# Gated scores with keys on partitions, made onto the turned probabilities, in a gated-attention and feed-forward layer

## The reference

```python
q, k, v = h @ Wq, h @ Wk, h @ Wv                   # h = layernorm(x); 32 heads of q, 8 of k and v, D = 128
qs, ks_ = softmax(q, -1), softmax(k, -1)
gs = log_sigmoid(k) / 16
# branch 1, a scan over all positions:
S = S * exp(g_t)[..., None] + k_t[..., None] * v_t[..., None, :];  o_t = q_t @ S
# branch 2: rope(q), rope(k), softmax over a sliding window (W = 64: own block and the one before)
x = x + layernorm((0.5 * y + 0.5 * o_lin) @ Wo)
# feed forward; every 64 values of w1, w2, w3 share one maximum
absmax = max(abs(w.reshape(-1, 64)), 1); n = w / where(absmax == 0, 1, absmax)
dq = NF4_CODE[searchsorted(bounds, n)] * absmax
x = x + layernorm((silu(hx @ dq1.T) * (hx @ dq2.T)) @ dq3.T)   # hx = layernorm(x)
```

## Time and profile before

| what | value |
|---|---|
| median of 3 runs | 1913.04 us (1912.93 to 1913.94) |
| the profiled execution's own time | 1912.8 us |
| its span | 1911.0 us |
| TensorE busy | 1834.3 us, 96% of the span |
| VectorE | 1484.2 us, 78% |
| ScalarE | 1278.5 us, 67% |
| GpSimd | 1264.8 us, 66% |
| DMA | 47 GB/s over the span |

### The profile page before, as it was taken

How to read it: one execution, slowest core, us unless ns; L and a number is a source line. 1 busy time by engine, 2 the same in 40 slices (tenths; PEclk the granted TensorE clock), 3 DMA queues, 4 the chain that set the end, 5 groups by cost and what they waited for, 6 DMA issues and landing times.

```text
span 1911.0 us, 42834 instructions
## 1 busy us (share of the span) xinstructions
PE 1834.3 (96%) x11439; PEld 1212.8 (63%) x11439; DVE 1484.2 (78%) x3980; ACT 1278.5 (67%) x4967; POOL 1264.8 (66%) x1164
## 2 busy tenths in 40 slices
PE   4899999999999999999999999999989999999997
PEld 3567667676777677667767776776666654444443
DVE  5999899999999888899998889999999956302112
ACT  5688777777777777777777777777677745312121
POOL 2767777777777777777777777777766738212121
PEclk8999999999999999999999999999999999999999
DMA  6101111111111111111111111111211033000000
GB/s 223 54 30 44 38 50 48 46 44 46 45 45 43 43 48 43 43 43 43 43 44 50 43 43 43 43 43 35 85 31 30 24 110 111 34 1 22 0 22 22
DMA packets 85452, 90.51 MB, mean 47 GB/s; under 512 B 14216, under 2 KB 56456, under 8 KB 85384
## 3 DMA queue, kind: packets, MB, share of 16 engines
q1 hardware_dynamic: 85384, 89.71, 15.2%
HBM read 76.48 MB, written 13.18 MB: 47 GB/s over the span
## 4 chain that ended last, share of the span: by engine, by line
PE 49%; DVE 23%; issue 19%; POOL 4%; ACT 2%; DVEq 1%; DMA 0%; POOLq 0%; ACTq 0%
PE bank L1369 12%; PE bank L1398 6%; PE bank L1358 5%; DVE f_s L1061 5%; PE bank L1340 4%; PE bank L1414 4%; PE bank L1496 3%; PE bank L1407 3%; PE bank L1435 3%; DVE f_nrm L1048 2%; PE bank L1324 2%; DVE qtT L961 2%; POOL hl L600 2%; PE bank L1514 2%; DVE qc L909 2%
## 5 line engine op out<-in xcount | busy, mean ns | idle before, releaser
L554 POOL TENSOR_TENSOR f_acc<-f_acc,f_s 128x512 f32<-128x512 f32 x429 | 548.9, 1279 | 32.6 <-POOL f_acc L554 0.4
L1369 PE MATMUL bank<-wh,xh 128*128 (+2 forms) x1024 | 335.0, 327 | 7.5 <-DVE cumh L1210 6.3
L1369 PE MATMUL bank<-wl,xh 128*128 (+2 forms) x1024 | 335.0, 327 | 0.0
L1369 PE MATMUL bank<-wh,xl 128*128 (+2 forms) x1024 | 334.8, 327 | 0.0
L1061 DVE TENSOR_SCALAR f_s<-f_nrm 128x512 f32<-128x512 f32 x480 | 282.1, 647 | 3.5
L538 POOL TENSOR_TENSOR pr<-pr,rp 128x512 f32<-128x512 f32 x128 | 133.3, 1041 | 216.1 <-DVE rp L983 216.1
L651 ACT ACTIVATE qe<-bank,nqm 128x128 f32<-128x128 f32 x512 | 180.9, 365 | 95.7 <-DVE qs L912 84.0
L1496 PE MATMUL bank<-xh,w 128*128 (+3 forms) x704 | 218.4, 379 | 1.7 <-ACT sg L837 1.7
L600 POOL TENSOR_TENSOR hl<-hf,hh 128x512 f16<-128x512 f32 (+1 forms) x44 | 51.3, 1167 | 231.4 <-ACT hh L843 231.4
L1220 DVE SCALAR_TENSOR_TENSOR hf<-bank,sg 128x512 f32<-128x512 f32 (+1 forms) x44 | 30.3, 689 | 221.5 <-PE bank L1496 210.6
L1358 PE MATMUL bank<-wh,oT 128*128 (+1 forms) x512 | 194.0, 379 | 4.4 <-DVE xl L1127 3.6
(11 more groups left out here) (179 smaller groups left out, 4918.9 us busy)
## 6 DMA issues: line engine op xcount, KB each, us to landing
f_blk<-wa SPq DMA_DIRECT2D x33, 320.0 KB, 2.9
f_raw<-wb SPq DMA_DIRECT2D x33, 256.0 KB, 2.7
dequantised<-f_w SPq DMA_DIRECT2D x33, 256.0 KB, 2.0
w<-dequantised SPq DMA_DIRECT2D x33, 256.0 KB, 4.3
raw_qkv<-wq SPq DMA_DIRECT2D x29, 256.0 KB, 2.4
raw_o<-wo SPq DMA_DIRECT2D x29, 256.0 KB, 2.6
f_recb<-scales SPq DMA_DIRECT2D x99, 64.0 KB, 2.6
f_absb<-scales SPq DMA_DIRECT2D x99, 64.0 KB, 2.6
```

The source lines that it names most:

```text
L554: nc.gpsimd.tensor_tensor(f_acc[:], f_acc[:], f_s[:, step, :], ALU.add).then_inc(s["f_ad"], 1)
L1369: last = nc.tensor.matmul(dst, av, w[:, sl + c, lo:hi], start=(n == 0), stop=(n == 3 * NC - 1))
```

## The change

The gated scores are made with keys on partitions and queries on columns, as the turned probabilities are. So they are added onto these by TensorE: the four transposes of `pr` open an accumulation in X1, and two products (keys as weights, 256 query columns each) add to it. The first takes its keys from `ktF`, a new tile that holds the first 64 keys of a tile and zeros behind them. `merge` becomes one product with a 0/1 mask from X1 to `pa`; the bias matmuls and `copy_pa` go, and ScalarE copies 64 columns more (`ktF`). `probabilities` moves from behind the state's update to ahead of `gla_scores`, which stands ahead of the turn of q as before; it waits for `softmax_p` and for the earlier `pa`. On VectorE `add_out` stands ahead of `merge`, and `nf4_end` behind `p_max`. `em` is made by ScalarE as exp(x + keep) with keep 0 or -1e30, ahead of the exponential of `ked` in the turn after a p = 0 tile. Each NF4 block gets a 65th value, the smallest normal fp32 number, and the instruction that replaced a zero maximum by 1 goes. Left out of the diff below: tiles, semaphores and start values (`cum` now lies in the staging tile; one more memset at the start, for `ktF`), and the same order of calls in the peeled last turns.

```diff
@@ -662,6 +664,9 @@
                 wait_tile(act, s["qt_d"], t, 2)
                 wait_tile(act, s["sr_d"], t, 1)
                 nc.scalar.activation(edT[:, r, :], SM[:, P:P + 130], ACT.Exp)
+                if t.p == 0 and not (isinstance(t.i, int) and t.i == 0):
+                    nc.scalar.activation(em[:, 0, :], SM[:, 2 * P:2 * P + 1], ACT.Exp,
+                                         bias=keep[:].unsqueeze(2)[:, t.i % 2, :])
                 nc.scalar.activation(ked, ked, ACT.Exp, scale=-1.0).then_inc(s["dec_ev"], 1)
 
             def mask_scores(t):
...
@@ -685,15 +690,10 @@
 
-            def copy_pa(t):
-                wait_tile(act, s["pt_done"], t)
-                wait_tile(act, s["o_done"], t, 2)
-                if number(t) == 0:
-                    act.wait_ge(s["wo_lo"], NC)
-                nc.scalar.activation(pa[:, t.p % 2, :], X1[:], ACT.Copy).then_inc(s["pa_ev"], 1)
-
             def copy_ktT(t):
                 wait_tile(act, s["ktT_done"], t)
+                wait_tile(act, s["at_done"], t, 1)
+                nc.scalar.activation(ktF[:, 0:WIN], SM[:, 0:WIN], ACT.Copy)
                 nc.scalar.activation(ktT[:, t.p % 2, :], SM[:, 0:P], ACT.Copy).then_inc(s["ktT_ev"], 1)
...
@@ -985,13 +982,10 @@
 
                 wait_tile(dve, s["at_done"], t)
-                wait_tile(dve, s["pn_p"], t)
-                v = pr[:, t.p % 2, :]
-                half = lambda a: a.rearrange("p (h n) -> p h n", h=GRP)[:, 0:2, 0:WIN]
-                nc.vector.scalar_tensor_tensor(out=half(v), in0=half(X1[:]), scalar=0.0, in1=half(v),
-                                               op0=ALU.max, op1=ALU.add)
-                nc.vector.scalar_tensor_tensor(out=v[:, 2 * P:], in0=X1[:, 2 * P:], scalar=0.0, in1=v[:, 2 * P:],
-                                               op0=ALU.max, op1=ALU.add).then_inc(s["pm_d"], 1)
+                wait_tile(dve, s["o_done"], t, 2)
+                if number(t) == 0:
+                    dve.wait_ge(s["wo_lo"], NC)
+                nc.vector.tensor_tensor(pa[:, t.p % 2, :], X1[:], cau[:], ALU.mult).then_inc(s["pa_ev"], 1)
 
             def state(t):
...
@@ -1003,9 +997,6 @@
                 if nxt.p == 0:
-                    nc.vector.tensor_tensor(em[:, 0, :], scale, keep[:, nxt.i % 2:nxt.i % 2 + 1] if isinstance(nxt.i, int)
-                                            else keep[:].unsqueeze(2)[:, nxt.i % 2, :], ALU.mult).then_inc(s["em_d"], 1)
-                    dve.wait_ge(s["em_d"], nxt.i)
                     scale = em[:, 0, :]
...
@@ -1026,15 +1017,10 @@
                     dve.wait_ge(s["f_rowd"], j)
-                nc.vector.tensor_reduce(f_col[:, 0:NF4_MAXIMA], f_blk[:].rearrange("p (b n) -> p b n", n=BLK), AX.X, ALU.max,
+                nc.vector.tensor_reduce(f_col[:, 0:NF4_MAXIMA], f_blk[:].rearrange("p (b n) -> p b n", n=GUARDED), AX.X, ALU.max,
                                         apply_absolute_value=True).then_inc(s["f_maxd"], 1)
                 dve.wait_ge(s["f_maxd"], j + 1)
-
-                nc.vector.scalar_tensor_tensor(out=f_safe[:], in0=f_col[:, 0:NF4_MAXIMA], scalar=0.0,
-                                               in1=f_col[:, 0:NF4_MAXIMA], op0=ALU.is_equal, op1=ALU.add)\
-                    .then_inc(s["f_safed"], 1)
-                dve.wait_ge(s["f_safed"], j + 1)
-                nc.vector.reciprocal(f_col[:, NF4_MAXIMA:2 * NF4_MAXIMA], f_safe[:]).then_inc(s["f_recd"], 1)
+                nc.vector.reciprocal(f_col[:, NF4_MAXIMA:2 * NF4_MAXIMA], f_col[:, 0:NF4_MAXIMA]).then_inc(s["f_recd"], 1)
 
...
@@ -1138,20 +1124,20 @@
                 if l1.real():
                     q_sums(l1)
-                if t.p == 1 and not (isinstance(t.i, int) and t.i == 0):
-                    nf4_end(t.i - 1)
                 if t.p == 2 and not (isinstance(t.i, int) and t.i == 0):
                     nf4_low(t.i - 1)
                 if l1.real():
                     gla_k(l1)
+                if l3.real():
+                    add_out(l3)
                 if l2.real():
                     merge(l2)
-                if l3.real():
-                    add_out(l3)
                 if l2.real():
                     state(l2)
                 if l1.real():
                     p_max(l1)
+                if t.p == 1 and not (isinstance(t.i, int) and t.i == 0):
+                    nf4_end(t.i - 1)
                 log_decay(t)
                 low_decay(t)
...
@@ -1328,18 +1314,11 @@
                 r = t.p % 2
                 wait_tile(pe, s["qt_d"], t)
                 wait_tile(pe, s["ktT_ev"], t)
-                wait_tile(pe, s["pa_ev"], t, 1)
-                half = lambda a: a.rearrange("p (h n) -> p h n", h=GRP)[:, 0:2, 0:WIN]
-                nc.tensor.matmul(half(X1[:]), identb[:], half(cau[:]), start=True, stop=False)
-                nc.tensor.matmul(X1[:, 2 * P:], identb[:], cau[:, 2 * P:], start=False, stop=False)
-                for b in range(2):
-
-                    keys = (b + 1) * WIN
-                    for hp in range(2):
-                        j = 2 * b + hp
-                        last = nc.tensor.matmul(X1[:, j * P:j * P + keys],
-                                                qtT[:, r, b, 2 * hp:2 * hp + 2, :].rearrange("p h n -> p (h n)"),
-                                                ktT[:, r, 0:keys], start=False, stop=(j == 3))
+                for b, keys in enumerate((ktF[:], ktT[:, r, :])):
+
+                    last = nc.tensor.matmul(X1[:, b * 256:(b + 1) * 256], keys,
+                                            qtT[:, r, b].rearrange("p h n -> p (h n)"),
+                                            start=False, stop=(b == 1), skip_group_check=True)
                 last.then_inc(s["at_done"], 1)
 
             def project_out(t):
...
@@ -1402,9 +1381,11 @@
                 r = t.p % 2
-                wait_tile(pe, s["pm_d"], t)
+                wait_tile(pe, s["pn_p"], t)
+                wait_tile(pe, s["pa_ev"], t, 1)
                 for j in range(GRP):
-                    last = nc.tensor.transpose(X1[:, j * P:(j + 1) * P], pr[:, r, j * P:(j + 1) * P], ident[:])
+                    last = nc.tensor.matmul(X1[:, j * P:(j + 1) * P], pr[:, r, j * P:(j + 1) * P], ident[:],
+                                            start=(j == 0), stop=False, is_transpose=True, skip_group_check=True)
                 last.then_inc(s["pt_done"], 1)
...
@@ -1454,12 +1435,12 @@
                 if l3.real():
                     project_out(l3)
                 if l2.real():
+                    probabilities(l2)
                     gla_scores(l2)
                 if l1.real():
                     turn_q(l1)
                 if l2.real():
                     inter_and_update(l2)
-                    probabilities(l2)
                 if l1.real():
                     scores(l1)
                 if x_tile_at(n):
...
@@ -1587,10 +1568,11 @@
-    n = np.arange(P)[:, None] % WIN
-    cau = np.zeros((P, 2, 2, P), np.float32)
-    for b in range(2):
-        cau[:, b] = np.where(n + b * WIN >= slot, 0.0, -3e38)[:, None, :]
+    key = np.arange(P)[:, None]
+    query = np.arange(WIN)[None, :]
+    cau = np.zeros((P, 2, GRP, WIN), np.float32)
+    cau[:, 0] = ((key >= WIN) | (query >= key))[:, None, :]
+    cau[:, 1] = (query + WIN >= key)[:, None, :]
...
@@ -1600,15 +1582,16 @@
-    keep = np.ones((P, 2), np.float32)
-    keep[:, 0] = 0.0
+    keep = np.zeros((P, 2), np.float32)
+    keep[:, 0] = MASKED
     return {"cosc": cos, "sinc": sin, "winmask": win, "causal": cau, "cumsum": cum,
             "identc": np.eye(P, dtype=np.float32), "keepc": keep}
 
 
 def feed_forward_pieces(w1, w2, w3):
 
-    by_block = np.zeros((NF4_PIECES, P, NF4_MAXIMA, BLK), np.float32)
+    by_block = np.zeros((NF4_PIECES, P, NF4_MAXIMA, GUARDED), np.float32)
+    by_block[..., BLK] = SMALLEST
```

More of the change, by code:

```diff
@@ L38 @@
 BLK = 64
+GUARDED = BLK + 1
+SMALLEST = float(np.finfo(np.float32).tiny)
 NF4_PIECE = 512
@@ L184, in layer @@
         win = sb("win", [P, 2, 512], BF16)
-        f_blk = sb("f_blk", [P, NF4_MAXIMA * BLK])
+        f_blk = sb("f_blk", [P, NF4_MAXIMA * GUARDED])
         f_raw = sb("f_raw", [P, NF4_PIECE])
@@ L196, in layer @@
         cau = sb("cau", [P, 512], BF16)
-        cum = sb("cum", [P, 130])
         cumh = sb("cumh", [P, 130], F16)
@@ L204, in layer @@
         ktT = sb("ktT", [P, 2, P])
+        ktF = sb("ktF", [P, P])
         krT = sb("krT", [P, 4, WIN])
@@ L218, in layer @@
         rp = sb("rp", [P, 2, GRP])
-        f_safe = sb("f_safe", [P, NF4_MAXIMA])
         PQ, PKV, X0, X1, SC, SM, PO, PW = bank
@@ L225, in layer @@
         stage = f_s[:].rearrange("p a n -> p (a n)")
+        cum = stage[:, 3840:3970]
         w_raw = [raw_qkv[:]] + [stage[:, 1536 + 768 * j:2304 + 768 * j] for j in range(NC - 1)]
@@ L246, in layer @@
             kmx_d nkm_a kabs_ev kneg_d krope_d g_d gl_d rks_d kt_d qmx_d nqm_a qrope_d rq_d qt_d pmx_d
-            rp_d pm_d pa_ev su_d em_d sr_d acc_d qrope_p krope_p qn_p pn_p
```

(25 more changed lines are left out.)

## The result

The changed kernel takes 1900.82 us (1900.40 to 1901.28, 4 runs), against 1912.99 us for the kernel before in the same session: ratio 0.9936, 95% interval 0.9918 to 0.9953. It is faster, by 12 us, and not by the 38 that were forecast. The profiled execution's span is 1898.6 us.

A forecast was written before the change was run, and what follows sets the result against it. TensorE's own work was taken to set the pace, with late VectorE adding about 1.1 us per four turns. Savings of 1.4 us in 24 steps (33.6), plus 3 and 1.5, gave 38 us: 1912.8 to 1875, range 1861 to 1894.

The forecast's parts named there:

- TensorE's work and order: Attention turn on TensorE: 0.20 us less, 11.29 to 11.09; gated scores' products in 0.87, wait for `qtT` at A+0.44.
- The new wait: VectorE, from p=3 to p=0: `gh` would wait 0.23 us for `kabs`.
- `em` on ScalarE: In p=1, `em` costs ScalarE 0.31 us, or up to 0.86, hidden behind its wait for the turn of q.
- `kt` in p=1: `kt` ends at A+2.0, or 2.3 with VectorE's later start, needed at 2.61: no TensorE stall.
- Ends: Turns outside the 24 steps: 3 us gained before 227 us and 1.5 in the last 15 turns.
- VectorE's work: VectorE per four turns: merge +0.07 us a turn, `em` -0.86, guard against zero -0.2; net -0.8 us.
- what becomes of the waits: Stalls per four turns: p=0 still loses 0.4 us, p=1 none; `nf4_end` delays L551, costing VectorE some 0.6 us.
- room: VectorE's waits for TensorE's scores, 0.46 us in 72 turns, taken as slack that absorbs lateness.
- The prediction's own sign of being wrong: Wrong if products exceed 0.95 us, `em` shows before `kt`, or VectorE no longer waits for scores in most turns.
- L551 holds VectorE: Rival: GpSimd's first sum blocks VectorE in p=1 for its whole 1.27 us; 14 us more, 1889 us; chance 0.08.
- only TensorE's work goes: Rival: ScalarE's chain, 0.25 us later every turn, eats what p=1 gives; gain 21 us, 1892 us; chance 0.18.

The follow-up runs named there:

- e12: Changed kernel with VectorE's threshold steps covering 8 of 512 columns from the second step of four turns on, GpSimd's sums all 512: 1863.79 us.
- e11: Changed kernel, nothing left out, with threshold steps reading 3 rows of 172 columns with gaps and writing one run of 516: 1852.81 us.
- e9: Kernel before the change with only `nf4_end` moved behind `pmx`: 1920.13 us.
- e3: Changed kernel with `nf4_end` put back ahead of `kt`: 1890.85 us.
- e1: Changed kernel with GpSimd's sums of the threshold steps cut to 8 of 512 columns: 1831.75 us.
- e10: Changed kernel with VectorE's threshold steps made a plain copy without two-port mode, thresholds left out: 1851.56 us.
- e13: Kernel before the change with threshold steps reading 3 rows with gaps and writing one run, nothing left out: 1946.51 us.

## Why the prediction was wrong, point by point

- *TensorE's work and order*: right. An unstalled turn is 11.09 us, the two products take 0.87.
- *The new wait, and `em` on ScalarE*: right, 0.22 us in 47 turns; `em` takes 0.30 us there and is hidden.
- *`kt` in p=1*: right. It runs from 837.00 us, A+2.0, to A+2.35 (forecast 2.3), and TensorE loses nothing in that turn.
- *Ends*: outside the 24 steps, 12.2 - 24 x 0.3 = 5 us were gained, 4.5 forecast. A small misreading: a step of before is 46.28 us and its fourth turn 11.29, not 46.32 and 11.33.
- *What failed is the step "VectorE's work"*, with "what becomes of the waits": the interval from `pmx` to the next `kmx` was taken over as 7.46 us, and the steps in it as a fixed price. It is 8.34 us now (815.55 to 823.89), where 7.46 and the new wait of 0.23 were expected, and it begins at A+4.23 and not 3.93. These 0.95 us are what lies between the 0.23 that the prediction had ahead of p=0 and the 1.18 that were lost. The dear price is that of meeting a sum of GpSimd, and VectorE's waits for the scores, which the prediction called room, were what pushed its steps behind the sums. The prediction's own sign of being wrong came true with that: VectorE no longer waits for the scores. With the scores earlier and that wait gone, the steps of p=2 and p=3 moved 1.2 and 0.6 us toward the sums and grew by 0.94 and 0.57 us. I priced this meeting for L551 alone: 0.6 us of VectorE a step, and it was 0.64; the other 1.7 of the 2.35 had no term. Part of it went into room that VectorE had; 1.1 us a step came out as time, 45.97 instead of 44.9, and 24 of them are the 26 us that are missing.
- *The rivals*: "L551 holds VectorE" had the right mechanism, in one turn of the three, and with 1889 us was 12 off; "only TensorE's work goes", with the wrong one, was 9 off. That it is an exclusion and not a slowing e12 shows. The trace of before held it too, in the ends of its 48 dear steps and of `em`, though none of the prediction's rows did. The Trainium skill's rule (SBUF — State Buffer, Who interferes with whom), that the later of the two blocks until the first has ended, agrees: 1.25 us for 8 columns, and `f_nrm` and GpSimd's rotation change places as payer with their order. Its condition agrees too: with the two-port mode of the steps prevented by outermost counts of 3 and 516 (the Trainium skill, VectorE: DVE Perf Modes, What auto-detection actually checks), e11 has one price.
- *Was it the scores' new order or `nf4_end`?* Both. The move costs 7 us alone (e9) and 10 on top of the rest (e3). e3 still misses the forecast by 16 us, as the steps of p=2 and p=3 stay at 2.82 and 4.02; e1, e10 and e11 take that away as well. Of the 94 us between e13 and e11, 68 are 24 x 2.8 in the steady steps, and some 11 more come from a turn of 15.06 instead of 13.39 us in 7 of these steps, whose cause stays open; the rest lies in the first and last turns and was not traced.

## What to carry to other kernels

A duration in a trace belongs to its neighbours as well: where two engines shut each other out, ask of every wait that a change removes what it kept apart, and price an instruction at both of its values. When one form of an instruction is half as fast but shares nothing, it can be the better one: steps of 0.61 us always, for 0.35 or over 1 (0.71 on average), were worth 48 us with what came of them. A small instruction with two SBUF operands is no small cost beside a busy GpSimd; look for it before a schedule is shifted.

## What the runs showed of the hardware

- A VectorE step of 512 columns, fp32, one SBUF source: 0.35 us from start to start alone, up to 1.52 us on record beside GpSimd's sums of 1.27 us, the longest of which took 1.45.
- One or ten columns of two SBUF operands: 0.15 and 0.17 us alone, 0.86 and 1.2 beside a sum.
- 512 columns of two SBUF operands on each engine: VectorE's 1.77 us and GpSimd's 1.26 where GpSimd started 0.04 us ahead, 0.77 and 1.74 where VectorE started 0.18 us ahead.
- A source in 3 rows with a gap and a destination in one run of 516: 0.61 us a step beside sums and alone (676 to 694 ns on record over 204 steps).
